# Two recurrent layers in series: the gate biases written by copies instead of products, side work moved between steps, two waits in exchanged order

## The chip, the cores and the metric

The kernel runs on one core of one Trainium2 chip. The metric is device microseconds of one execution, from the first to the last instruction with what lies around them; of several executions the median counts.

## The reference

What must be computed, in float32, with x of 16 batches, 128 time steps and 128 features:

```python
def lstm(x, h0, Wx, Wh, b):            # twice, with weights of its own
    x_proj = einsum('ntd,df->ntf', x, Wx) + b
    def step(carry, xp_t):
        prev_h, prev_c = carry
        h_bar = xp_t + prev_h @ Wh     # four gates of 128
        i, f, o = sigmoid(h_bar[:, :H]), sigmoid(h_bar[:, H:2*H]), sigmoid(h_bar[:, 2*H:3*H])
        g = tanh(h_bar[:, 3*H:])
        next_c = f * prev_c + i * g
        next_h = o * tanh(next_c)
        return (next_h, next_c), next_h
    ...
x = x + attention(lstm(x, cond, ...), W_theta, W_phi, W_g)   # no softmax: theta phi^T scaled, times g
x = x + relu(lstm(x, cond, ...) @ W1 + b1) @ W2 + b2
```

The second layer's input is the first layer's output plus its attention, so the two recurrences of 128 steps each stand one after the other: 256 dependent steps.

## The kernel before

**Layout.** Features lie on the partitions, and the 16 batches of a time step are 16 columns. Eight time steps make a chunk of 128 columns (`CH` = 8); a layer has 16 chunks. Two chunks (16 steps, parities p = 0 and 1) are one turn of a loop: `pe.Fori`, `act.Fori` and `dve.Fori` on the three engines. Layer 1 is eight turns of its loop. Layer 2's first 16 steps are written out (they also carry the rest of the attention), and seven turns follow. In the code t is the step within its chunk and s the step within 16.

**Gate banks.** Each parity has two banks of PSUM: `gibank[p]` holds gates g and i of the chunk's eight steps, `fobank[p]` gates f and o. While the steps of one parity run, the other parity's banks are filled: first the bias by float32 products of a matrix of ones with a 128x512 bias matrix that has the bias in row 0 and zeros below (`bias_gate`, L350 to L353; the products for gates f and g carry start=True), then the input part x @ Wx by one float32 product per gate (`project_gate`, L355 to L358). Each step adds its recurrent part onto the step's 16 columns.

**One step.** TensorE (`step`, L371): a float32 product of the last h (`ring`) with gate f's weights (L387, after h_ready), six half-precision products of `h_hi` and six of `h_lo` for gates g and i (L377), then, after ScalarE has read gate f, six for gate o. ScalarE: sigmoid of f (L662), tanh of g and i (L665), sigmoid of o (L669), tanh of the cell (L672). VectorE: f times the cell (L746), the scan that forms the new cell (L750), h (L753), its half-precision part `h_hi` (L755) and remainder `h_lo` (L758). The scan waits for two things, ScalarE's gates g and i, and VectorE's own product f times the cell:

```python
dve.wait_ge(gi_done[layer], n1)
dve.wait_ge(fc_done[layer], n + 2)
nc.vector.tensor_tensor_scan(out=c_scan, ...)
```

**Side work.** The order on each engine is the order in which the code is written; nothing else schedules. After the 19 products of a step TensorE does that step's piece of other work and then waits for the next h: in layer 1 the transposing of the next chunk's x and the products for values and keys (t = 0), bias products (one at t = 0, three at t = 1), queries (t = 2), input products (one at t = 2, three at t = 3), scores (t = 4), attention (t = 6). In layer 2's loop it is the feed-forward products and, at t = 2, 3, 6 and 7, one bias product and one input product. `keep_warm` (L360) adds dummy half-precision products of 512 columns, as many as the tables say:

```python
WARM1 = [0, 0, 0, 0, 1, 3, 1, 3]
WARM2 = [1, 1, 0, 1, 1, 1, 1, 1]
```

VectorE's side work stands behind L758 of a step (scores L763 at t = 5, a copy L782 at t = 7, in layer 2 relu L809 at t = 2 and 3 and the output L849 at t = 6), ScalarE's behind L672.

**Start.** SyncE loads x, bias and condition of layer 1, ScalarE's queue its weights, GpSimd's queue all of layer 2's, which GpSimd then scales and splits until about 22 us. VectorE scales gate g's part of bias, `Wh` and `Wx` and splits `Wh` (L732 to L741).

## Time and profile before

| | us |
|---|---|
| median of 3 runs (all: 485.89, 489.92, 499.64) | 489.92 |
| the profiled execution | 489.24 |
| its span, first to last instruction | 487.2 |

| engine | busy us | share of the span |
|---|---|---|
| TensorE products | 451.1 | 93% |
| TensorE weight loads | 354.8 | 73% |
| VectorE | 261.3 | 54% |
| ScalarE | 212.8 | 44% |
| GpSimd | 17.4 | 4% |

The times of a row are start and duration in microseconds from the span's start. A float32 product of 128 columns stands in the trace as two records of weight load and two of product, so "x4" is two products. Products overlap in the array: their starts tell how long it is taken, their durations do not. "PEld" is the weight load, "PE" the product, "DVEq" VectorE's own queue (waits and register arithmetic), and what stands in brackets is the idle time of the engine ahead of the row and who ended it. The granted clock reads 1.00 in every stretch of this trace.

### The profile page before, as it was taken

How to read it: one execution, taken by the hardware profiler on the slowest of the kernel's cores; microseconds unless marked ns; L12 is line 12 of the kernel's file. 1: busy time of each engine (PE TensorE's matmuls, PEld its weight loads, DVE VectorE, ACT ScalarE, POOL GpSimd, SP SyncE). 2: the span in 40 equal slices, each digit the busy share in tenths (PEclk: the TensorE clock that was granted, in tenths of full speed). 3: DMA queues.
4: the chain of work that ended last, by engine and by line, in shares of the span. 5: the costliest groups of instructions: out<-in, count | busy, mean ns of one | idle time of the engine just before them, and what ended most of it. 6: DMA issues, size and time to landing. Idle time of an engine off the chain costs nothing.

```text
span 487.2 us, 16863 instructions
## 1 busy us (share of the span) xinstructions
PE 451.1 (93%) x6350; PEld 354.8 (73%) x6440; DVE 261.3 (54%) x1422; ACT 212.8 (44%) x1092; POOL 17.4 (4%) x29
## 2 busy tenths in 40 slices
PE   8999999999999999999999999999999999999997
PEld 6876677766667776667789977777777777777775
DVE  4445554555555455555545655555555555555554
ACT  1434445444454444444435344444444444444443
POOL 6700000000000000000000000000000000000000
PEclk9999999999999999999999999999999999999999
DMA  5001111001111100110000000000000000000000
GB/s 160 7 3 17 16 16 16 14 3 16 16 16 16 16 11 5 16 16 11 11 12 3 7 18 18 18 16 12 4 16 16 16 16 16 11 5 16 16 16 11
DMA packets 11690, 8.12 MB, mean 17 GB/s; under 512 B 1098, under 2 KB 11130, under 8 KB 11675
## 3 DMA queue, kind: packets, MB, share of 16 engines
q1 hardware_dynamic: 10874, 6.17, 6.4%
q0 software_dynamic: 512, 1.22, 0.8%
q10 hardware_dynamic: 288, 0.52, 0.4%
q8 instruction: 10, 0.16, 0.2%
q14 instruction: 6, 0.04, 0.0%
HBM read 2.87 MB, written 1.05 MB: 8 GB/s over the span
## 4 chain that ended last, share of the span: by engine, by line
PE 60%; DVE 16%; ACT 14%; issue 7%; DVEq 1%; DMA 1%; ACTq 0%
PE fobank L387 20%; PE gibank L377 16%; DVE cell L750 10%; ACT scan L665 8%; DVE ring L753 6%; ACT cell L672 6%; PE fobank L377 5%; PE gibank L352 3%; PE fobank L352 3%; PE gibank L357 3%; PE fobank L357 2%; PE bankY L431 2%; DVEq L749 1%; PE bankY L535 1%; DMA x_rows<-in_x_dram 1%
## 5 line engine op out<-in xcount | busy, mean ns | idle before, releaser
L387 PEld LDWEIGHTS fobank<-ring,whf 128*128 128x128 f32 x510 | 78.3, 192 | 96.7 <-DVE ring L753 96.3
L387 PE MATMUL fobank<-ring,whf 128*128 128x16 f32 x510 | 100.1, 272 | 28.5 <-DVE ring L753 19.0
L662 ACT ACTIVATE fgate<-fobank 128x16 f32<-128x16 f32 x256 | 47.2, 184 | 167.6 <-PE fobank L387 165.3
L750 DVE TENSOR_TENSOR_SCAN cell<-scan 128x48 f32<-128x48 f32 x256 | 69.1, 270 | 56.2 <-ACT scan L665 53.1
L746 DVE TENSOR_TENSOR scan<-fgate,cell 128x16 f32<-128x16 f32 x256 | 45.4, 177 | 90.4 <-ACT fgate L662 88.4
L377 PEld LDWEIGHTS gibank<-h_hi,wh_parts 128*128 128x128 bf16 x1536 | 79.6, 111 | 0.0
L753 DVE SCALAR_TENSOR_TENSOR ring<-cell,ogate 128x16 f32<-128x16 f32 x256 | 44.7, 175 | 60.0 <-ACT cell L672 60.0
L377 PE MATMUL gibank<-h_hi,wh_parts 128*128 128x16 f16 x1536 | 75.5, 169 | 0.0
L377 PE MATMUL gibank<-h_lo,wh_parts 128*128 128x16 f16 x1536 | 75.4, 169 | 0.0
L665 ACT ACTIVATE scan<-gibank 128x32 f32<-128x32 f32 x256 | 54.9, 215 | 27.9
L672 ACT ACTIVATE cell<-cell 128x16 f32<-128x16 f32 x256 | 43.0, 168 | 40.6 <-DVE cell L750 38.8
L377 PE MATMUL fobank<-h_hi,wh_parts 128*128 128x16 f16 x771 | 60.0, 174 | 0.4 <-ACT fgate L662 0.2
L377 PEld LDWEIGHTS gibank<-h_lo,wh_parts 128*128 128x128 bf16 x1536 | 56.6, 96 | 0.0
L377 PE MATMUL fobank<-h_lo,wh_parts 128*128 128x16 f16 x768 | 56.2, 169 | 0.0
L669 ACT ACTIVATE ogate<-fobank 128x16 f32<-128x16 f32 x256 | 47.1, 184 | 19.9 <-PE fobank L377 0.5
L377 PEld LDWEIGHTS fobank<-h_hi,wh_parts 128*128 128x128 bf16 x771 | 36.2, 97 | 19.5 <-ACT fgate L662 0.5
L758 DVE TENSOR_TENSOR h_lo<-ring,h_hi 128x16 f16<-128x16 f32 x256 | 45.2, 176 | 8.7
L755 DVE SCALAR_TENSOR_TENSOR h_hi<-cell,ogate 128x16 f16<-128x16 f32 x256 | 42.2, 165 | 0.0
L377 PEld LDWEIGHTS fobank<-h_lo,wh_parts 128*128 128x128 bf16 x768 | 37.4, 96 | 0.0
L363 PE MATMUL bankU<-warm_x,warm_w 128*128 128x512 bf16 x96 | 29.7, 392 | 1.3 <-issue 0.2
L352 PE MATMUL fobank<-ones,bias 128*128 128x128 f32 x136 | 28.6, 293 | 0.0
L352 PE MATMUL gibank<-ones,bias 128*128 128x128 f32 x136 | 27.7, 310 | 0.0
(150 smaller groups left out, 467.8 us busy)
## 6 DMA issues: line engine op xcount, KB each, us to landing
rows_t<-rows SPq DMA_DIRECT2D x16, 128.0 KB
x_rows<-in_x_dram SPq DMA_DIRECT2D x17, 64.0 KB
out_dram<-y_sb SPq DMA_DIRECT2D x16, 64.0 KB
xres<-x2T SPq DMA_DIRECT2D x15, 64.0 KB, 1.9
xin<-x2T SPq DMA_DIRECT2D x14, 64.0 KB, 1.8
w<-in_L_ffn_W_dram POOLq DMA_DIRECT2D x2, 256.0 KB, 3.9
wh<-in_L_cond_Wh_dram ACTq DMA_DIRECT2D x1, 256.0 KB, 2.8
wx<-in_L_cond_Wx_dram ACTq DMA_DIRECT2D x1, 256.0 KB, 3.7
```

What stands on the lines that cost most here:

```text
L352: return nc.tensor.matmul(gate_out(p, g), bias[layer][:, gate_cols(g)], moving(ones[:, :], g), start=g in (GF, GG), stop=False, skip_group ...
L377: last = nc.tensor.matmul(step_out(p, t, g), wh_parts[layer][:, part, gate_cols(g)], h[:, (s - 1) % STEPS, :], start=False, stop=True, ski ...
L387: nc.tensor.matmul(step_out(p, t, GF), whf[layer][:], ring[:, (s - 1) % STEPS, :], start=False, stop=True, skip_group_check=True).then_inc ...
L662: nc.scalar.activation(fgate[:], fobank[p][:, NB * t:NB * t + NB], ACT.Sigmoid).then_inc(f_done[layer], 1)
L665: nc.scalar.activation(gi_slots, gibank[p][:, 2 * NB * t:2 * NB * (t + 1)].rearrange("p (g b) -> p g b", g=2), ACT.Tanh, scale=0.5).then_i ...
L669: nc.scalar.activation(ogate[:], fobank[p][:, P + NB * t:P + NB * t + NB], ACT.Sigmoid).then_inc(tanh_done[layer], 1)
L672: nc.scalar.activation(tanhc, c_psum, ACT.Tanh, scale=0.5).then_inc(tanh_done[layer], 1)
L746: nc.vector.tensor_tensor(out=fc_slots, in0=fgate[:], in1=c_psum, op=ALU.mult).then_inc(fc_done[layer], 1)
L750: nc.vector.tensor_tensor_scan(out=c_scan, data0=scan_mul, data1=scan_add, initial=0.0, op0=ALU.mult, op1=ALU.add).then_inc(c_ready[layer], 1)
L753: nc.vector.scalar_tensor_tensor(out=ring[:, s, :], in0=tanhc, scalar=H_UNIT, in1=ogate[:], op0=ALU.mult, op1=ALU.mult).then_inc(h_ready[l ...
L755: nc.vector.scalar_tensor_tensor(out=h_hi[:, s, :], in0=tanhc, scalar=H_UNIT, in1=ogate[:], op0=ALU.mult, op1=ALU.mult).then_inc(hi_ready[ ...
L758: nc.vector.tensor_tensor(out=h_lo[:, s, :], in0=ring[:, s, :], in1=h_hi[:, s, :], op=ALU.subtract).then_inc(lo_ready[layer], 1)
```

## The change

Bias: the two matrices of 128x512 become two of 128x4, one column a gate (order g, i, f, o), loaded by two DMAs each (`load_bias`), layer 1's on SyncE's queue with no clearing ahead, layer 2's on GpSimd's. `bias_gate`, `ones` and all bias products are gone. In their place VectorE writes the bias into the other parity's banks with two copies of 128x256 from SBUF to PSUM (`seed_gi`, `seed_fo`), and TensorE's input products wait for them (`seeded`). Where they stand: layer 1 behind steps t = 1 and t = 2; layer 2's loop behind t = 0 and t = 1; in the written-out 16 steps both behind step 1 and both behind step 11; before each layer's first step, both. The four dummy products at the start now write the gate banks.

Side work on TensorE: in layer 1 the products for values and keys move from t = 0 to t = 1 and the input products from t = 2 (one) and t = 3 (three) to t = 3 (two) and t = 5 (two). In the written-out steps the four input products at step 12 move to steps 13 (one), 14 (one) and 15 (two). `WARM1` and `WARM2` are the same.

The scan's two waits stand in the other order.

```diff
@@ VectorE, step @@
                 nc.vector.tensor_tensor(out=fc_slots, in0=fgate[:], in1=c_psum,
                                         op=ALU.mult).then_inc(fc_done[layer], 1)
+                dve.wait_ge(fc_done[layer], n + 2)
                 dve.wait_ge(gi_done[layer], n1)
-                dve.wait_ge(fc_done[layer], n + 2)
                 nc.vector.tensor_tensor_scan(out=c_scan, data0=scan_mul, data1=scan_add, initial=0.0,
...
@@ VectorE, new functions and the loop of layer 1 @@
+            def seed_gi(layer, p):
+                nc.vector.tensor_copy(gibank[p][:, 0:2 * P].rearrange("p (t g b) -> p t g b", g=2, b=NB),
+                                      bias[layer][:, 0:2].unsqueeze(1).unsqueeze(3).broadcast_to([P, CH, 2, NB])
+                                      ).then_inc(seeded[layer], 1)
+            def seed_fo(layer, p):
+                nc.vector.tensor_copy(fobank[p][:, 0:2 * P].rearrange("p (g n) -> p g n", g=2),
+                                      bias[layer][:, 2:4].unsqueeze(2).broadcast_to([P, 2, P])
+                                      ).then_inc(seeded[layer], 1)
...
+                    if t == 1:
+                        seed_gi(0, 1 - p)
+                    if t == 2:
+                        seed_fo(0, 1 - p)
...
@@ VectorE, before the first step @@
-            dve.wait_ge(bias1_loaded, 16)
-            nc.vector.tensor_scalar(bias[0][:, gate_cols(GG)], ...)
+            dve.wait_ge(bias1_loaded, 32)
+            nc.vector.tensor_scalar(bias[0][:, 0:1], bias[0][:, 0:1], 2.0, None, ALU.mult).then_inc(bias_ready, 1)
+            dve.wait_ge(gate_banks_opened, 1)
+            dve.wait_ge(bias_ready, 1)
+            seed_gi(0, 0)
+            seed_fo(0, 0)
             dve.wait_ge(wh1_loaded, 16)
...
@@ loads @@
+        def load_bias(eng, layer, b, done):
+            eng.dma_start(bias[layer][:, 1:4], b[0:3 * H].rearrange("(g p) -> p g", p=P), ...).then_inc(done, 16)
+            eng.dma_start(bias[layer][:, 0:1], b[3 * H:4 * H].unsqueeze(1), ...).then_inc(done, 16)
...
@@ TensorE, loop of layer 1 @@
+                    if t == 1:
                         pe.wait_ge(rows_kept, i * 2 + (p + 1))
                         row_products(1 - p, bankY)
-                    if t in (0, 1):
-                        for g in (GATES[0:1], GATES[1:])[t]:
-                            bias_gate(0, 1 - p, g)
...
+                    if t in (3, 5):
+                        if t == 3:
+                            pe.wait_ge(seeded[0], i * 4 + (2 * p + 4))
+                        rhs = xT[:, bass.ds(i * 2 + (p + 1), 1), :].rearrange("p c n -> p (c n)")
+                        for g in {3: GATES[0:2], 5: GATES[2:4]}[t]:
+                            project_gate(0, 1 - p, g, rhs)
...
-                    if t in (2, 3):
-                        rhs = ...
-                        for g in (GATES[0:1], GATES[1:])[t - 2]:
-                            project_gate(0, 1 - p, g, rhs)
...
@@ TensorE, layer 2, written-out steps @@
-                if s in (8, 9, 10, 11):
-                    bias_gate(1, 0, GATES[s - 8])
...
-                    for g in GATES:
+                if s in (13, 14, 15):
+                    if s == 13:
+                        pe.wait_ge(seeded[1], 6)
+                    for g in {13: GATES[0:1], 14: GATES[1:2], 15: GATES[2:4]}[s]:
                         last = project_gate(1, 0, g, x2T[:, 2, :])
...
@@ TensorE, loop of layer 2 @@
                         g = {2: GF, 3: GG, 6: GI, 7: GO}[t]
-                        bias_gate(1, 1 - p, g)
+                        if t == 2:
+                            pe.wait_ge(seeded[1], i * 4 + (2 * p + 4))
                         last = project_gate(1, 1 - p, g, xin[:, 1 - p, :])
```

**The scan's waits, in VectorE's row.** A wait is either a part of the instruction it stands with or an instruction of its own ahead of it. The kernel before, a looped step of layer 1 (`cell<-scan` is the scan, REGISTER_ALU the arithmetic for a wait's value):

```order
L758 TENSOR_TENSOR h_lo<-ring,h_hi 128x16 [waits hi_ready1]
L746 TENSOR_TENSOR scan<-fgate,cell 128x16 [waits f_done1]
L749 REGISTER_ALU [waits gi_done1]
L750 SCALAR_TENSOR_TENSOR cell<-scan 128x48 [waits fc_done1]
L752 ISA
L753 SCALAR_TENSOR_TENSOR ring<-cell,ogate 128x16 [waits tanh_done1]
```

The changed kernel, behind step t = 1 of layer 1:

```order
L767 TENSOR_TENSOR h_lo<-ring,h_hi 128x16 [waits hi_ready1]
L715 COPY gibank<-bias 128x256
L755 TENSOR_TENSOR scan<-fgate,cell 128x16 [waits f_done1]
L757 REGISTER_ALU
L759 SCALAR_TENSOR_TENSOR cell<-scan 128x48 [waits gi_done1,fc_done1]
L761 ISA
L762 SCALAR_TENSOR_TENSOR ring<-cell,ogate 128x16 [waits tanh_done1]
```

Before, the register arithmetic (L749) waits for gates g and i, and the scan for f times the cell. Now the arithmetic waits for nothing, and two waits stand with the scan. Of two in such a list the first named is an instruction of its own ahead (L758, a bare semaphore wait) and the last is the scan's own: it is again f times the cell. In the written-out steps of the kernel before the list is the other way round:

```order
L758 TENSOR_TENSOR h_lo<-ring,h_hi 128x16 [waits hi_ready2]
L763 TENSOR_TENSOR scores<-bankY,same_batch 128x256 [waits scores_ready]
L746 TENSOR_TENSOR scan<-fgate,cell 128x16 [waits f_done2]
L750 SCALAR_TENSOR_TENSOR cell<-scan 128x48 [waits fc_done2,gi_done2]
L753 SCALAR_TENSOR_TENSOR ring<-cell,ogate 128x16 [waits tanh_done2]
```

and in the changed kernel it is as in the loop:

```order
L767 TENSOR_TENSOR h_lo<-ring,h_hi 128x16 [waits hi_ready2]
L772 TENSOR_TENSOR scores<-bankY,same_batch 128x256 [waits scores_ready]
L755 TENSOR_TENSOR scan<-fgate,cell 128x16 [waits f_done2]
L759 SCALAR_TENSOR_TENSOR cell<-scan 128x48 [waits gi_done2,fc_done2]
L762 SCALAR_TENSOR_TENSOR ring<-cell,ogate 128x16 [waits tanh_done2]
```

So outside the loop the wait for gates g and i moves from the scan itself to an instruction ahead of it.

**TensorE at t = 5 of layer 1.** Before, from the step's last products for gate o to the next step's first product:

```order
L377 MATMUL fobank<-h_hi,wh_parts 128x16 x2
L377 MATMUL fobank<-h_lo,wh_parts 128x16 x3
L363 MATMUL bankU<-warm_x,warm_w 128x512 x3
L386 REGISTER_ALU
L387 MATMUL fobank<-ring,whf 128x16 [waits h_ready1]
```

And now:

```order
L373 MATMUL fobank<-h_hi,wh_parts 128x16 x2
L373 MATMUL fobank<-h_lo,wh_parts 128x16 x3
L353 MATMUL gibank<-xT,wx 128x8x16
L353 MATMUL fobank<-xT,wx 128x128
L359 MATMUL bankU<-warm_x,warm_w 128x512 x3
L382 REGISTER_ALU
L383 MATMUL fobank<-ring,whf 128x16 [waits h_ready1]
```

Two input products now stand ahead of the three dummy ones.

## Rows read from the trace of the kernel before

**Rows 1.** The page, part 4: the chain that ended last, shares by engine
```profile
PE 60%; DVE 16%; ACT 14%; issue 7%; DVEq 1%; DMA 1%; ACTq 0%
```

**Rows 2.** Timeline, a looped step of layer 1 (start us, us, what)
```profile
104.77 0.17 DVE L753 SCALAR_TENSOR_TENSOR ring<-cell,ogate 128x16 f32<-128x16 f32 x1 [0.23 <-ACT cell L672]
...
105.00 0.30 PEld L387 LDWEIGHTS fobank<-ring,whf 128*128 128x128 f32 x2 [0.18 <-DVE ring L753]
...
105.65 0.18 DVE L746 TENSOR_TENSOR scan<-fgate,cell 128x16 f32<-128x16 f32 x1 [0.41 <-ACT fgate L662]
...
105.81 0.52 PEld L352 LDWEIGHTS gibank<-ones,bias 128*128 128x128 f32 x4
...
106.06 0.27 DVE L750 TENSOR_TENSOR_SCAN cell<-scan 128x48 f32<-128x48 f32 x1 [0.23 <-ACT scan L665]
...
106.26 0.30 PEld L352 LDWEIGHTS fobank<-ones,bias 128*128 128x128 f32 x2
...
106.56 0.17 DVE L753 SCALAR_TENSOR_TENSOR ring<-cell,ogate 128x16 f32<-128x16 f32 x1 [0.23 <-ACT cell L672]
...
106.79 0.30 PEld L387 LDWEIGHTS fobank<-ring,whf 128*128 128x128 f32 x2 [0.23 <-DVE ring L753]
```

**Rows 3.** Source line L749, VectorE's queue: duration ns min/median/max, first and last start
```profile
L749 DVEq ALU_OP  x233: 40/40/52, 13.8 to 481.1; - x117
L749 DVEq EVENT_SEMAPHORE  x23: 21/21/21, 251.0 to 479.3; - x23
```

**Rows 4.** Chain in order of time, a looped step (start us, us, what)
```profile
112.88 0.22 ACT scan L665
...
113.14 0.04 DVEq L749
...
113.22 0.28 DVE cell L750
```

**Rows 5.** Chain in order of time, a step of layer 2 outside the loop
```profile
254.24 0.22 ACT scan L665
...
254.48 0.28 DVE cell L750
```

**Rows 6.** Chain in order of time, the last products and the last copy
```profile
483.16 0.96 PE bankY L531 x8
...
484.15 0.02 DVEq L855
...
484.22 0.29 DVE y_sb L856
```

**Rows 7.** Timeline, layer 1, the step with t = 5
```profile
112.99 0.81 PE L363 MATMUL bankU<-warm_x,warm_w 128*128 128x512 bf16 x3
113.95 0.30 PEld L387 LDWEIGHTS fobank<-ring,whf 128*128 128x128 f32 x2 [0.64 <-DVE ring L753]
```

**Rows 8.** Timeline, layer 2, step 12 outside the loop: two results
```profile
276.48 0.17 DVE L753 SCALAR_TENSOR_TENSOR ring<-cell,ogate 128x16 f32<-128x16 f32 x1 [0.23 <-ACT cell L672]
...
278.40 0.17 DVE L753 SCALAR_TENSOR_TENSOR ring<-cell,ogate 128x16 f32<-128x16 f32 x1 [0.23 <-ACT cell L672]
```

**Rows 9.** Groups by line and shape (busy us, mean ns | idle before)
```profile
L763 DVE TENSOR_TENSOR scores<-bankY,same_batch 128x256 f32<-128x256 f32 x17 | 7.2, 425 | 0.0
```

**Rows 10.** Timeline, VectorE, early steps of layer 1
```profile
20.15 0.17 DVE L753 SCALAR_TENSOR_TENSOR ring<-cell,ogate 128x16 f32<-128x16 f32 x1 [0.23 <-ACT cell L672]
...
22.17 0.17 DVE L753 SCALAR_TENSOR_TENSOR ring<-cell,ogate 128x16 f32<-128x16 f32 x1 [0.23 <-ACT cell L672]
...
24.49 0.17 DVE L753 SCALAR_TENSOR_TENSOR ring<-cell,ogate 128x16 f32<-128x16 f32 x1 [0.23 <-ACT cell L672]
```

**Rows 11.** Timeline, before the first step
```profile
5.82 0.55 PEld L352 LDWEIGHTS fobank<-ones,bias 128*128 128x128 f32 x2 [0.28 <-issue]
...
8.08 0.50 PEld L357 LDWEIGHTS fobank<-xT,wx 128*128 128x128 f32 x2
```

**Rows 12.** DMA issues by line (KB, us from issue to landing)
```profile
b<-in_L_ffn_b_dram POOLq DMA_DIRECT2D x1, 2.0 KB, 3.5
```

More of the change, by code:

```diff
@@ L75, in build @@
         ident = sb("ident", [P, P])
-        ones = sb("ones", [P, P])
         wx = [sb(f"wx{n}", [P, 4 * H]) for n in (1, 2)]
         wh = [sb(f"wh{n}", [P, 4 * H]) for n in (1, 2)]
-        bias = [sb(f"bias{n}", [P, 4 * H]) for n in (1, 2)]
+        bias = [sb(f"bias{n}", [P, 4]) for n in (1, 2)]
         cond_rows = sb("cond_rows", [NB, H])
@@ L224, in start_h @@
             nc.vector.memset(c_psum, 0.0).then_inc(fc_done[layer], 1)
+        def load_bias(eng, layer, b, done):
+            eng.dma_start(bias[layer][:, 1:4], b[0:3 * H].rearrange("(g p) -> p g", p=P),
+                          allow_slow_non_contiguous=True).then_inc(done, 16)
+            eng.dma_start(bias[layer][:, 0:1], b[3 * H:4 * H].unsqueeze(1),
+                          allow_slow_non_contiguous=True).then_inc(done, 16)
         @block.sync
@@ L229, in _ @@
             sp.dma_start(x_rows[:, 0, :], x_ctb[0]).then_inc(rows_loaded[0], 16)
-            sp.wait_ge(bias1_cleared, 1)
-            sp.dma_start(bias[0][0:1, :], l1_b.unsqueeze(0)).then_inc(bias1_loaded, 16)
+            load_bias(sp, 0, l1_b, bias1_loaded)
             sp.dma_start(cond_rows[:], cond).then_inc(cond_loaded, 16)
@@ L304, in _ @@
             pool.dma_start(wg_rows[:], w_g).then_inc(attn_w_loaded, 16)
-            nc.gpsimd.memset(bias[1][:], 0.0).then_inc(bias2_cleared, 1)
-            pool.wait_ge(bias2_cleared, 1)
-            pool.dma_start(bias[1][0:1, :], l2_b.unsqueeze(0)).then_inc(weights2_loaded, 16)
+            load_bias(pool, 1, l2_b, weights2_loaded)
             pool.dma_start(wx[1][:], l2_wx).then_inc(weights2_loaded, 16)
@@ L315, in _ @@
             nc.gpsimd.memset(x2T[:, NCH, :], 0.0).then_inc(set2_ready, 1)
-            pool.wait_ge(weights2_loaded, 112)
-            for w in (wx[1], wh[1], bias[1]):
-                nc.gpsimd.tensor_scalar(w[:, gate_cols(GG)], w[:, gate_cols(GG)], 2.0, None,
-                                        ALU.mult).then_inc(set2_ready, 1)
+            pool.wait_ge(weights2_loaded, 128)
+            for w in (wx[1][:, gate_cols(GG)], wh[1][:, gate_cols(GG)], bias[1][:, 0:1]):
+                nc.gpsimd.tensor_scalar(w, w, 2.0, None, ALU.mult).then_inc(set2_ready, 1)
             nc.gpsimd.tensor_scalar(w1[:], w1[:], 1.0 / H_UNIT, None, ALU.mult).then_inc(set2_ready, 1)
@@ L348, in moving @@
                 return tile if g in (GF, GO) else tile.rearrange("p (t b) -> p t b", b=NB)
-            def bias_gate(layer, p, g):
-                return nc.tensor.matmul(gate_out(p, g), bias[layer][:, gate_cols(g)], moving(ones[:, :], g),
-                                        start=g in (GF, GG), stop=False, skip_group_check=True)
             def project_gate(layer, p, g, tile):
@@ L399, in _ @@
             pe.wait_ge(consts_ready, 1)
-            keep_warm(bankV, 4)
+            for bank in (gibank[0], fobank[0], gibank[1], fobank[1]):
+                last = nc.tensor.matmul(bank[:, :], warm_w[:], warm_x[:], start=True, stop=True, skip_group_check=True)
+            last.then_inc(gate_banks_opened, 1)
             pe.wait_ge(consts_ready, 2)
@@ L477, in _ @@
             pe.wait_ge(set2_ready, SET2)
-            for g in GATES:
-                bias_gate(1, 0, g)
             last_keys = ring[:, CH:STEPS, :].rearrange("p t b -> p (t b)")
@@ L544, in _ @@
                     score_products(P, hist[:, 0, :], P, P).then_inc(scores_ready, 1)
-                if s == 1:
-                    for g in GATES:
-                        bias_gate(1, 1, g)
                 if s == 2:
@@ L576, in _ @@
                     residual(x2T[:, 0, :])
-                    for g in GATES:
+                if s in (13, 14, 15):
+                    if s == 13:
+                        pe.wait_ge(seeded[1], 6)
+                    for g in {13: GATES[0:1], 14: GATES[1:2], 15: GATES[2:4]}[s]:
                         last = project_gate(1, 0, g, x2T[:, 2, :])
+                if s == 15:
                     last.then_inc(x2_projected, 1)
@@ L784, in _ @@
                                               ).then_inc(hist_done, 1)
+            dve.wait_ge(set2_ready, SET2)
+            seed_gi(1, 0)
+            seed_fo(1, 0)
             dve.wait_ge(scores_ready, NCH + 1)
@@ L816, in _ @@
                     keep_scores(2 * P)
+                if s == 1:
+                    seed_gi(1, 1)
+                    seed_fo(1, 1)
                 if s == 2:
@@ L820, in _ @@
                     late_x2(s - 7)
+                if s == 11:
+                    seed_gi(1, 0)
+                    seed_fo(1, 0)
                 if s == 12:
@@ L837, in _ @@
                     c = i * 2 + p
+                    if t == 0:
+                        seed_gi(1, 1 - p)
+                    if t == 1:
+                        seed_fo(1, 1 - p)
                     if t == 2:
```

15 lines of the change are left out of this document (5 added, 10 removed).

## The prediction, made before the changed kernel ran

> **What bounds the kernel now.** I read the chain that ended last first: TensorE has 60% of it, VectorE 16%, ScalarE 14% [rows 1]. That a busy engine is also the bound is not said by this, so the timeline of one step came next. From one h (L753) to the next the step takes 1.79 us, 104.77 to 106.56 [rows 2], and the reader is to see two things in it. The load for L387 stood idle for 0.23 us until VectorE's h came, though three bias products had been made in that step; so TensorE waits for h even in a full step. And the scan L750 stood idle for 0.23 us until ScalarE's gates g and i came. The ring h, L387, gates, scan, tanh, h is the bound, and side work is not, as long as it fits between gate o's products and the next h. Reading all results of L753 in order, 119 of layer 1's steps and 105 of layer 2's are 1.79 us long. So 0.01 us in the ring is worth over 2 us, and 50 us of products outside it are worth nothing.
>
> **The change, part by part.**
>
> *The scan's waits.* In a looped step ScalarE's gates end at 113.10, the register arithmetic that waits for them starts at 113.14 and the scan at 113.22: 0.12 us from gates to scan [rows 4]. Outside the loop, where the scan itself waits for the gates and a bare wait ahead of it takes the other semaphore, it is 254.46 to 254.48, 0.02 to 0.03 us [rows 5]. After the change it is neither: a bare wait for the gates, then the scan. This combination the trace shows at the end, for the last copy: the products end at 484.12, the bare wait starts at 484.15, the copy at 484.22, which is 0.10 us [rows 6]. The queue's durations say the same: 40 ns for the arithmetic, 21 ns for a bare wait, a difference of 0.019 us [rows 3]. That arithmetic stood there 233 times: 233 x 0.019 = 4.4 us gained. The other 23 steps (16 written out, one in each of 7 turns) had the good form and lose it: 0.10 - 0.03 = 0.07 us in about 18 of them, while in about 5 the product f times the cell comes last and gains as much: 1.3 - 0.4 = 0.9 us lost. Sum -3.5 us. Bounds: nothing gained in the 233 and all 23 lost, +1.6; or the gates' wait as fast as in rows 5, -21.
>
> *Bias products.* All of them go. In rows 2 the three took TensorE from 105.81 to about 106.48, and the next load waited for h all the same: worth 0 in the loops. The cover was the wait itself, so nothing is uncovered either.
>
> *The copies.* A copy of 128x256 with PSUM on one side: the nearest row is the product for the scores, 0.43 us of the same size [rows 9]. It stands behind L758, where VectorE has 0.41 us of idle time before L746 [rows 2], so L746 starts at most a few hundredths late; L746 ends 0.23 us before the scan starts (105.83, 106.06) [rows 2], and the scan's own wait for it needs 0.03 of that. Up to about 0.6 us a copy costs 0. In the written-out steps 1 and 11 two stand in a row: 0.86 us, L746 0.45 late, of which 0.2 is slack: +0.25 each, +0.5 us. From below: a copy like the fastest of its size, 0.3 us, gives 0.
>
> The Trainium skill (VectorE: DVE Perf Modes, section "Why PSUM operands drop a tier") says that a float32 operation with a PSUM operand gets no double rate. The trace's 0.43 us agrees as an estimate of one element a cycle. By the double rate the copies would take some 0.3 us and these 0.5 us would be 0.
>
> *Layer 1's step t = 5.* The input products move behind three dummy products' step. Before, the dummies took TensorE from 112.99, some 0.215 us each (0.81 us with the last one's tail), and the next step's load began at 113.95 [rows 7]. Two float32 products take 0.45 us more (105.81 to 106.26 for two) [rows 2]: the array is free at 112.99 + 0.45 + 0.64 = 114.08, against a load that would now start at 113.93 and may run beside the last dummy for some 0.1 us. So 0.05 to 0.15 us. The nearest row of a step with five such pieces is step 12 outside the loop, 1.92 us [rows 8], against 1.70 for its neighbours, which had less; that was a float32 tail, whose loads are longer. I take 0.1: 16 x 0.1 = +1.6 us; bounds 0 and 16 x 0.22 = 3.5. In no other step is there more than three pieces, and four fitted at 1.70.
>
> *The first steps.* Step times there: 20.15 to 22.17 is 2.02 us, with the side work hidden; 22.17 to 24.49 is 2.32 us with three input products [rows 10]. The products' durations there are twice those of later stretches, the lower level of TensorE's two, though the granted clock reads 1.00. Steps 1 and 3 go from three pieces to two (-0.3 each), step 0 from three and a half to a transposing (-0.6), step 5 from three to five at twice 0.215 (+0.86): -0.4 us. GpSimd's operations stall VectorE here now and then, up to 0.8 us, and where they fall then cannot be said: bounds -2 and +1.
>
> *Before the first step.* The bias products run from 5.82 on, the input products start at 8.08 [rows 11]. Now the latter wait for the copies. Layer 1's bias comes in single elements; layer 2's b1, of 2 KB in single elements too, took 3.5 us from issue to landing [rows 12]. Issued at about 1.6 and 2.3, the bias is there at 5.8; doubling gate g's column, two copies (0.86), then `Wh` and `Wx` scaled: the input products start at about 7.4, -0.7 us. Bounds: -1.5, and +2 if the load takes 2.7 us longer, since nothing else would cover it.
>
> *Between the layers and in the written-out steps.* Before the second layer the products with h0 now wait for two copies behind the last h, where bias products filled TensorE: +0.35 us. Steps 8 to 11 lose one bias product each behind attention products that keep TensorE busy: 0.22 to 0.3 us in three of them, -0.8 us. Bounds -1.5 and +1 for both.
>
> *Sum.* -3.5 + 0 + 0.5 + 1.6 - 0.4 - 0.7 + 0.35 - 0.8 = -2.95 us. The profiled execution took 489.24 us (its span 487.2 and 2.0 around it), so 486.3 us. The three runs' median is 0.14% above that execution: 487.0 us. One per cent is 4.9 us; a measurement of this kernel tells about 2% from no change.
>
> **Rivals.**
>
> *The clock falls in layer 1's light steps (slower).* Before, each step had three pieces of side work of 0.215 to 0.22 us; now layer 1's t = 0 to 3 have half a piece, two, two and two, 7 us in a row of lighter work in each chunk. If TensorE falls to 1.2 GHz in them and comes back in the full steps t = 5 to 7, then t = 2 and 3 cost 2.02 instead of 1.79 [rows 10, 2], t = 4 about 2.4, t = 5 about 2.95, t = 6 about 2.33: up to 2.7 us a chunk, 43 us in 16. If only two light steps are hit, 0.46 x 16 = 7 us. That is 494 to 530, with 510 in between; from 0.6 us a chunk on it decides. For it: the early steps, which are full of products, still ran at the lower level until about 31 us, so rising is not easy. Against: no stretch after that fell, and some of those had gaps too.
>
> The Trainium skill (TensorE: Matmul & The Clock Gate, section "A second HAM failure mode: psum-queue depth-cycling") tells of a kernel whose frequent small gaps between groups made the clock swing between its two levels; by that the rival is right. The same page's section "Loop structure matters more than you think" ties the fall to long idle waits, which this kernel has not; by that it is wrong. No row here is as light as the new steps, so the trace bears out neither.
>
> *The exchange gives its full worth (faster).* If a wait ahead of the scan cost no more than the scan's own, the 0.12 would become 0.03: 233 x 0.09 = 21 us, so 469 us with the other terms. Rows 5 speak for it, but there the late semaphore was the scan's own; rows 6 have the new order and say 0.10.
>
> *The bias arrives late.* With the load's bound of +2 us and a stall of GpSimd's, 490 us: no measurable change either.
>
> **How the numbers follow.** The forecast has 0.68, with its own range of 482 to 492; the falling clock 0.22, of which 0.03 stay under 2%; the full exchange 0.05; the late bias 0.05. The range for all, 479 to 508, leaves out the full exchange and the worse half of the falling clock. Faster by over 2% (below 480): 0.06. Slower by over 2% (above 499.7): 0.19. Between: 0.75.
>
> **What would show it.** Right: the scan starts 0.10 us after ScalarE's gates in every step, looped steps are 1.77 us long, t = 5 of layer 1 1.85 to 1.9, L753 to L387's load keeps its idle time, copies last about 0.43 us and L746 is not followed by a late scan. Wrong: scans 0.03 us behind the gates (469); product durations of the light steps twice as long (over 494); scans that wait for L746; a first step that starts later than before.

## The result and the profile after

The changed kernel takes 572.23 us (median of 4 runs, 570.54 to 576.49) against 490.14 for the kernel before beside it: 1.174 times as long, 95% interval 1.164 to 1.185. The forecast was 487.0 with a range of 479 to 508. The profiled execution took 572.85 us, its span 570.7. Throughout, a time is the median of all executions of a kernel, while a ratio leaves out those in a slower state of the chip, so the two can differ by some tenths of a per cent.

The page of the changed kernel: busy time, granted clock in 40 slices, and the chain by engine.

```profile
PE 546.1 (96%) x6168; PEld 443.0 (78%) x6168; DVE 286.5 (50%) x1488; ACT 211.8 (37%) x1092; POOL 17.1 (3%) x29
PEclk9997756557756557756688675555556655556656
PE 88%; DVE 5%; ACT 3%; issue 2%; DMA 1%; DVEq 0%; ACTq 0%
```

Before, PEclk was 9 in all slices and TensorE had 60% of the chain [rows 1]. Now TensorE runs mostly at the lower of its two levels (1.2 GHz; 5 in this line) and has 88%: the ring is no longer the only bound, TensorE's own products are.

Where the 83.5 us lie (570.7 - 487.2) is read from four results h each: the first, the first of layer 2's written-out steps, the first of its loop, the last. First before, then after.

```profile
14.41 0.17 DVE L753 SCALAR_TENSOR_TENSOR ring<-cell,ogate 128x16 f32<-128x16 f32 x1 [0.23 <-ACT cell L672]
...
251.57 0.17 DVE L753 SCALAR_TENSOR_TENSOR ring<-cell,ogate 128x16 f32<-128x16 f32 x1 [0.23 <-ACT cell L672]
...
283.60 0.18 DVE L753 SCALAR_TENSOR_TENSOR ring<-cell,ogate 128x16 f32<-128x16 f32 x1 [0.23 <-ACT cell L672]
...
481.69 0.17 DVE L753 SCALAR_TENSOR_TENSOR ring<-cell,ogate 128x16 f32<-128x16 f32 x1 [0.23 <-ACT cell L672]
```

```profile
13.75 0.17 DVE L762 SCALAR_TENSOR_TENSOR ring<-cell,ogate 128x16 f32<-128x16 f32 x1 [0.23 <-ACT cell L668]
...
291.52 0.17 DVE L762 SCALAR_TENSOR_TENSOR ring<-cell,ogate 128x16 f32<-128x16 f32 x1 [0.23 <-ACT cell L668]
...
327.57 0.17 DVE L762 SCALAR_TENSOR_TENSOR ring<-cell,ogate 128x16 f32<-128x16 f32 x1 [0.23 <-ACT cell L668]
...
564.45 0.17 DVE L762 SCALAR_TENSOR_TENSOR ring<-cell,ogate 128x16 f32<-128x16 f32 x1 [0.23 <-ACT cell L668]
```

Layer 1 with the hand-over: 277.77 against 237.16, +40.6. Written-out steps: 36.05 against 32.03, +4.0. Layer 2's loop: 236.88 against 198.09, +38.8. The rest +0.1.

How it comes in one chunk of layer 1: the changed kernel's windows from one h to the next; the side work of t = 0 stands in the first, that of t = 5 begins in the sixth and reaches into the last (length; busy time of PE, PEld, DVE, ACT, POOL; granted clock; DMA).

```profile
64.10:65.87 1.77, 1.24 (x22) 0.88 (x21) 1.05 (x7) 0.75 (x4) 0.00 (x0) 1.00 0.00 0
65.87:67.64 1.77, 1.51 (x22) 1.03 (x22) 0.87 (x5) 0.78 (x5) 0.00 (x0) 1.00 0.00 0
67.64:69.64 2.00, 1.77 (x22) 1.49 (x22) 1.22 (x7) 1.02 (x6) 0.00 (x0) 0.54 0.00 0
69.64:71.63 1.99, 1.99 (x25) 1.71 (x24) 1.21 (x7) 1.03 (x6) 0.00 (x0) 0.50 0.10 18
71.63:73.62 1.99, 1.99 (x25) 1.84 (x25) 0.88 (x5) 1.00 (x5) 0.00 (x0) 0.50 0.59 80
73.62:75.95 2.33, 2.33 (x26) 1.91 (x25) 0.88 (x5) 0.75 (x4) 0.00 (x0) 0.50 0.01 1
75.95:79.13 3.18, 3.18 (x28) 2.33 (x27) 1.23 (x7) 0.75 (x4) 0.00 (x0) 0.50 0.00 0
```

At t = 0 TensorE is busy for 1.24 of 1.77 us, at t = 1 for 1.51, then the clock falls. From there its own products fill the steps, and the five pieces of t = 5 make the last window 3.18 us long. In the kernel before the fullest and the lightest step of a chunk are these:

```profile
104.77:106.56 1.79, 1.79 (x29) 1.53 (x27) 0.88 (x5) 0.76 (x5) 0.00 (x0) 1.00 0.00 0
...
111.93:113.72 1.79, 1.56 (x23) 0.95 (x23) 0.88 (x6) 0.75 (x4) 0.00 (x0) 1.00 0.16 13
```

TensorE's waits for h in these steps are short. Its loads for the ring at t = 0, 1 and 2:

```profile
64.33 0.30 PEld L383 LDWEIGHTS fobank<-ring,whf 128*128 128x128 f32 x2 [0.62 <-DVE ring L762]
66.09 0.30 PEld L383 LDWEIGHTS fobank<-ring,whf 128*128 128x128 f32 x2 [0.82 <-DVE ring L762]
67.87 0.50 PEld L383 LDWEIGHTS fobank<-ring,whf 128*128 128x128 f32 x2 [0.66 <-DVE ring L762]
```

The same in groups: the load of `whf` for the ring (190 ns at the higher level, in fill_all below) takes half as long again, the dummy products more than a third (392 ns in the kernel before, last line below); the copies are as forecast.

```profile
L383 PEld LDWEIGHTS fobank<-ring,whf 128*128 128x128 f32 x510 | 132.6, 293 | 89.2 <-DVE ring L762 73.2
...
L359 PE MATMUL bankU<-warm_x,warm_w 128*128 128x512 bf16 x129 | 57.0, 536 | 0.0
...
L715 DVE COPY gibank<-bias 128x256 f32<-128x256 f32 x34 | 14.3, 421 | 0.1
```

```profile
L363 PE MATMUL bankU<-warm_x,warm_w 128*128 128x512 bf16 x96 | 29.7, 392 | 1.3 <-issue 0.2
```

What the change did to the scan's waits answers to [rows 4]: the chain of the changed kernel in a looped step.

```profile
65.06 0.22 ACT scan L661
65.28 0.03 issue
65.30 0.02 DVEq L758
65.33 0.04 issue
65.37 0.28 DVE cell L759
```

The gates end at 65.28, the scan starts at 65.37: 0.09 to 0.10 us, where it was 0.12.

### The profile page after: what moved, and what is told of

It is laid out like the page before. It is cut to its first block, busy times and chain, and to the rows that moved or that the text cites. A ratio compares the mean times of both kernels' runs of the same rounds, so it can differ in the third digit from the quotient of the medians.

```text
span 570.7 us, 16742 instructions
## 1 busy us (share of the span) xinstructions
PE 546.1 (96%) x6168; PEld 443.0 (78%) x6168; DVE 286.5 (50%) x1488; ACT 211.8 (37%) x1092; POOL 17.1 (3%) x29
## 4 chain that ended last, share of the span: by engine, by line
PE 88%; DVE 5%; ACT 3%; issue 2%; DMA 1%; DVEq 0%; ACTq 0%
PE fobank L383 14%; PE gibank L373 14%; PE fobank L373 11%; PE bankV L359 7%; PE bankU L359 7%; PE gibank L353 6%; PE fobank L353 6%; PE bankY L526 6%; PE bankU L519 5%; PE bankY L432 3%; PE bankU L453 3%; DVE cell L759 2%; PE bankV L437 2%; ACT scan L661 2%; DVE ring L762 2%
## 5 line engine op out<-in xcount | busy, mean ns | idle before, releaser
L383 PEld LDWEIGHTS fobank<-ring,whf 128*128 128x128 f32 x510 | 132.6, 293 | 89.2 <-DVE ring L762 73.2
L383 PE MATMUL fobank<-ring,whf 128*128 128x16 f32 x510 | 119.7, 314 | 16.9 <-DVE ring L762 15.2
L373 PEld LDWEIGHTS gibank<-h_hi,wh_parts 128*128 128x128 bf16 x1536 | 101.5, 129 | 0.0
L373 PE MATMUL gibank<-h_lo,wh_parts 128*128 128x16 f16 x1536 | 77.9, 173 | 0.4 <-DVE h_lo L767 0.4
L373 PE MATMUL fobank<-h_hi,wh_parts 128*128 128x16 f16 x771 | 63.4, 179 | 0.2 <-ACT fgate L658 0.2
L359 PE MATMUL bankV<-warm_x,warm_w 128*128 128x512 bf16 x104 | 62.5, 604 | 0.0
L373 PEld LDWEIGHTS gibank<-h_lo,wh_parts 128*128 128x128 bf16 x1536 | 59.7, 102 | 0.5 <-DVE h_lo L767 0.5
L359 PE MATMUL bankU<-warm_x,warm_w 128*128 128x512 bf16 x129 | 57.0, 536 | 0.0
L373 PEld LDWEIGHTS fobank<-h_hi,wh_parts 128*128 128x128 bf16 x771 | 40.1, 107 | 16.4 <-ACT fgate L658 0.3
L526 PE MATMUL bankY<-w,relu 128*128 128x128 f32 x128 | 36.7, 441 | 0.0
```

Of the source, the lines that this page charges most:

```text
L359: nc.tensor.matmul(bank[:, :], warm_w[:], warm_x[:], start=True, stop=True)
L373: last = nc.tensor.matmul(step_out(p, t, g), wh_parts[layer][:, part, gate_cols(g)], h[:, (s - 1) % STEPS, :], start=False, stop=True, ski ...
L383: nc.tensor.matmul(step_out(p, t, GF), whf[layer][:], ring[:, (s - 1) % STEPS, :], start=False, stop=True, skip_group_check=True).then_inc ...
L526: return nc.tensor.matmul(bankY[:, 0:D], relu[:, j, :], w2[:, j, :], start=False, stop=(j == NJ - 1))
```

## The experiments

All 17 kernels compute the whole reference; what is added or left out are dummy products and clearings, whose results nobody reads, and the form of a wait. Each ratio is to the kernel before, run beside it; us of a ratio are taken at 487. The granted clock is told by windows of the span; those of all runs stand in a table at the end.

**fill_both, fill_1, fill_2: is it the clock, and where?** Dummy products come back where bias products went.

```diff
 # these four lines: fill_both, fill_1
 t == 0:  +keep_warm(bankU, 2)
 t == 1:  +keep_warm(bankY, 1)
 t == 2:  +keep_warm(bankU, 1)
 t == 3:  +pe.wait_ge(rows_kept, i * 2 + (p + 2)); keep_warm(bankY, 1)
 # this line: fill_both, fill_2
-WARM2 = [1, 1, 0, 1, 1, 1, 1, 1]
+WARM2 = [1, 1, 1, 2, 1, 1, 2, 2]
```

> The changed kernel, and nothing taken back, with dummy products added where bias products were dropped: in layer 1 two more at t = 0 and one more at each of t = 1, 2 and 3; in layer 2 one more at each of t = 2, 3, 6 and 7. Theory (the 83 us come from TensorE's lower clock, and that from the lighter steps): the granted clock reads about 1.00 again, looped steps are 1.77 us, the time is 484 to 489 us. Rival A (the copies into the gate banks, or a wait for them, slow the ring whatever the clock does): the time stays above 540 us. Rival B (the clock falls because of t = 5 with its five pieces or of gaps before h, not of light steps): clock stays under 0.9 and the time above 520 us.

> The changed kernel with the dummy products of fill_both in layer 1's steps only; layer 2's steps stay as light as the change made them. Theory (each layer's own light steps pull the clock down): layer 1 at 1.00 with steps of 1.77 us, layer 2 at about 0.57 as in the changed kernel: 487 + some 105 x 0.38 = about 527 us, 520 to 535. Rival (layer 2 fell only because the clock was already low when it began, its own steps would hold it): under 495 us.

> The changed kernel with one dummy product more in layer 2's t = 2, 3, 6 and 7 only; layer 1 and the written-out steps stay as light as the change made them. Theory (each stretch pays for its own light steps): layer 1 and the written-out steps run mostly at the lower level as in the changed kernel, layer 2's loop at 1.00 and 1.77 us: 572 less the 38 us that the loop loses in fill_1 against fill_both = about 534, 526 to 542. Rival (once low, the clock doesn't come back in layer 2 though its steps are full): over 560.

Measured: fill_both 492.22 us, 1.013 (1.005 to 1.020); fill_1 529.82 us, 1.093 (1.086 to 1.099); fill_2 538.65 us, 1.107 (1.100 to 1.114). Some 78 us of 83 are gone once work that nobody needs is back. Each layer pays for itself: layer 2's filling is worth (1.093 - 1.013) x 487 = 39 us, layer 1's (1.107 - 1.013) x 487 = 46, and the stages above had lost 38.8 and 40.6 + 4.0. The copies and the waits for them are all still in fill_both, so rival A falls; so does rival B, whose five pieces at t = 5 are there too. The lines of PEclk, fill_both, fill_1 and fill_2:

```profile
PEclk9999999999999999999965589999999999999999
```

```profile
PEclk9899999999999999999898555555565556655656
```

```profile
PEclk9977556576657755756675598999999999999999
```

fill_both was expected at 484 to 489; a low stretch is left, at some 246 to 287 us: the hand-over and the written-out steps. These 16 steps take 41.23 us there and 36.05 in the changed kernel, by the same code, so what a light stretch costs isn't a fixed sum.

**fill_all, fill_all_t5: the rest, and the change at an even clock.** Both have fill_both's dummy products and these besides.

```diff
+keep_warm(bankU, 4)                    # before the hand-over's scores
+if s == 1: pe.wait_ge(rows0_kept, 1); keep_warm(bankU, 3)
 s == 12:  +keep_warm(bankV, 2)
-if s >= 13: keep_warm(bankV, 1 + 2 * (s == 15))
+if s >= 13: keep_warm(bankV, 2)
-WARM1 = [0, 0, 0, 0, 1, 3, 1, 3]       # fill_all_t5 alone
+WARM1 = [0, 0, 0, 0, 1, 1, 1, 3]
```

> fill_both, with dummy products also where the change left the hand-over and the written-out steps of layer 2 light: four before the hand-over's scores, three in step 1, two in step 12, two in each of steps 13 to 15. Theory (fill_both's clock fell at about 247 us because that stretch too had become lighter): clock 1.00 throughout, about 10 us less than fill_both: 480 to 484 us, level with the kernel that only exchanges the waits. Rival (the stretch fell for another reason, the wait for the copies behind the last h or the products of float32): the clock falls there again, 490 to 494.

> fill_all with one dummy product in place of three at layer 1's t = 5, so that its step has three pieces and not five. Theory (forecast: the two extra pieces cost 0.1 us a chunk at the higher level; the trace of fill_both shows 1.91 against 1.77, 0.14): t = 5 goes to 1.77 us, 2.2 us less than fill_all: ratio to before about 0.995. Rival (that step becomes one light step too many): the clock falls in part of layer 1, over 490 us.

Measured: fill_all 488.06 us, 0.999 (0.995 to 1.004), where 480 to 484 was expected and swap_only (below) has 0.993; the profiled execution took 484.66 us (span 482.5), clock 1.00 in all slices. fill_all_t5 485.29 us, 0.999 (0.995 to 1.003): two pieces less at t = 5 can't be told from none, and its profiled run lost the clock for a stretch in the written-out steps (0.83 from 240 to 290 us), so its 2 us are not resolved in the time. They are in the trace: the step behind t = 5 reads 1.77 us there. What it costs with five pieces is read from fill_all's h at t = 5 and after it: 224.69, 226.59, 228.36, so 1.90 against 1.77.

```profile
224.69 0.17 DVE L772 SCALAR_TENSOR_TENSOR ring<-cell,ogate 128x16 f32<-128x16 f32 x1 [0.23 <-ACT cell L678]
226.59 0.17 DVE L772 SCALAR_TENSOR_TENSOR ring<-cell,ogate 128x16 f32<-128x16 f32 x1 [0.23 <-ACT cell L678]
228.36 0.17 DVE L772 SCALAR_TENSOR_TENSOR ring<-cell,ogate 128x16 f32<-128x16 f32 x1 [0.23 <-ACT cell L678]
```

The load at the higher level, in the same kernel:

```profile
L383 PEld LDWEIGHTS fobank<-ring,whf 128*128 128x128 f32 x510 | 78.7, 190 | 112.8 <-DVE ring L772 110.1
```

**light_2, dose_1, uneven_2: light steps in the kernel before.** One row is changed, so that t = 3, 6 and 7 of layer 2's loop have two pieces where all had three; or t = 3 alone; or the three, with the pieces moved to t = 0, 1 and 4.

```diff
-WARM2 = [1, 1, 0, 1, 1, 1, 1, 1]
+WARM2 = [1, 1, 0, 0, 1, 1, 0, 0]    # light_2
+WARM2 = [1, 1, 0, 0, 1, 1, 1, 1]    # dose_1
+WARM2 = [2, 2, 0, 0, 2, 1, 0, 0]    # uneven_2
```

> The kernel before, nothing of the change, with one dummy product less in steps t = 3, 6 and 7 of layer 2's looped chunks (0.2 us of TensorE's work in each, none of it on the way to h). Theory (light steps alone do it): layer 2's granted clock falls below 0.8, its steps to 2.0 to 2.4 us, the time is 505 to 535 us, layer 1 unchanged. Rival (products outside the ring are worth nothing, and what fell was something else of the change): 488 to 491 us, clock 1.00.

> The kernel before with one dummy product less in one step of eight of layer 2's loop, t = 3, so that t = 3 has two pieces and every other step three. Theory A (a light step now and then is enough): the clock falls in part of layer 2, 495 to 520 us. Theory B (it takes several light steps in a row or near each other): 486 to 490, clock 1.00.

> The kernel before, layer 2's loop with as many dummy products as before (six in eight steps plus the one moved: 2, 2, 0, 0, 2, 1, 0, 0 where it was 1, 1, 0, 1, 1, 1, 1, 1), so that t = 3, 6 and 7 are as light as in light_2, and t = 0, 1 and 4 have four pieces. Theory A (light steps pull the clock down wherever the rest stands): as light_2, 505 to 535 us. Theory B (what counts is the work over the whole chunk): clock 1.00, 486 to 491 us.

Measured: light_2 521.67 us, 1.075 (1.067 to 1.083); dose_1 509.26 us, 1.043 (1.035 to 1.052); uneven_2 509.87 us, 1.037 (1.027 to 1.046). PEclk of light_2 and of dose_1:

```profile
PEclk9979999999999999999999995675555955655569
```

```profile
PEclk9699999999999999999999999555596989557969
```

One dummy product of 0.2 us less in every eighth step costs 21 us in a kernel that has nothing else of the change. Work elsewhere in the chunk doesn't make up for it (uneven_2), though it lessens the loss.

**swap_only, own_wait: the scan's waits.** In own_wait the count of gi_done starts 3 higher, so that a new value is worked out between the two waits: that arithmetic takes the wait for the product f times the cell, and the scan itself the one for the gates.

```diff
 # swap_only                            # own_wait, looped steps
-dve.wait_ge(gi_done[layer], n1)        -dve.wait_ge(gi_done[layer], n1)
 dve.wait_ge(fc_done[layer], n + 2)      dve.wait_ge(fc_done[layer], n + 2)
+dve.wait_ge(gi_done[layer], n1)        +dve.wait_ge(gi_done[layer], n + 4)
                                         # after start_h: +dve.sem_inc(gi_done[layer], 3)
```

> The kernel before with the scan's two waits exchanged and nothing else. Step by step forecast: 0.12 us between gates and scan become 0.10 in 233 steps, 23 steps lose 0.07: -3.5 us, 486.6. Rival A (full worth, 0.03 us as in the written-out steps): 469. Rival B (nothing, or a loss in the written-out steps alone): 490 to 491.5.

> The kernel before, where the scan in the looped steps waits itself for the gates (register arithmetic ahead of it takes the wait for the product f times the cell), in place of the arithmetic waiting for the gates; nothing else. Theory (what counts is which wait the scan itself has): 0.12 us between gates and scan become 0.03, steps 1.70 us, 233 x 0.09 = 21 us less: 465 to 469. Rival (the next thing to be late fills the gap: the product f times the cell, or the dummy products that reach up to the next h): steps stay at 1.75 or more, over 480.

Measured: swap_only 481.98 us, 0.993 (0.989 to 0.998), so -3.3 us (-5.4 to -1.2). own_wait 467.06 us, 0.955 (0.947 to 0.963), so -22 us. It beats both kernels. Its gates and scans (ScalarE, then VectorE):

```profile
322.49 0.21 ACT L665 ACTIVATE scan<-gibank 128x32 f32<-128x32 f32 x1
```

```profile
321.03 0.27 DVE L755 TENSOR_TENSOR_SCAN cell<-scan 128x48 f32<-128x48 f32 x1
...
321.53 0.18 DVE L758 SCALAR_TENSOR_TENSOR ring<-cell,ogate 128x16 f32<-128x16 f32 x1 [0.23 <-ACT cell L672]
...
322.74 0.27 DVE L755 TENSOR_TENSOR_SCAN cell<-scan 128x48 f32<-128x48 f32 x1
...
323.24 0.17 DVE L758 SCALAR_TENSOR_TENSOR ring<-cell,ogate 128x16 f32<-128x16 f32 x1 [0.23 <-ACT cell L672]
```

From 322.71 to 322.74 is 0.03 us, and from h to h 1.71.

**Fewer products, or more idle time?** own_dose_1 and own_light_2 are own_wait with the rows of dose_1 and light_2. gap_2 and gap_2b leave all products and put a clearing on VectorE before h in layer 2's looped steps; own_gap_light_2 is own_light_2 with that clearing.

```diff
 dve.wait_ge(tanh_done[layer], n * 2 + 2)
+if layer == 1 and not isinstance(n, int):
+    nc.vector.memset(spare[:], 0.0)     # 128x16 in gap_2, 128x128 in the others
```

> own_wait with dose_1's one light step (t = 3 of layer 2's loop has two pieces, the others three). With own_wait's steps of 1.70 TensorE's idle time before each h is 0.09 us shorter, so over eight steps it is 0.7 us shorter, and the piece left out adds 0.2 us of it in one. Theory A (what counts is how long TensorE stands idle over several steps): the clock holds at 1.00, the time is that of own_wait, 464 to 470. Theory B (what counts is the work of a single step): the clock falls in part of layer 2 as in dose_1, 478 to 495.

> The kernel before, all its products in place, with a clearing of a spare tile (128x16) on VectorE between tanh and h in each of the 112 looped steps of layer 2: h comes some 0.06 to 0.1 us later, and TensorE stands idle that much longer in every step. Theory A (TensorE's idle time over several steps is what pulls the clock down): besides the 7 to 11 us of the clearing itself the clock falls in layer 2's loop, over 505 us. Theory B (it is the number of products in a step): clock 1.00, steps of 1.85 to 1.9 us, 493 to 498.

> own_wait with light_2's three light steps of eight (t = 3, 6 and 7 of layer 2's loop with two pieces). Over eight steps the pieces left out add 0.6 us of idle time and own_wait's shorter steps take 0.7 us away. Theory A (idle time over several steps): the clock holds or falls only here and there, 464 to 475. Theory B (three light steps of eight are too many at any length of the ring): the clock falls as in light_2, over 490.

> gap_2 with a clearing of 128x128 in place of 128x16 (in gap_2 the 0.07 us of it ran beside the step and h came no later, so that it told nothing). Before's clearing of this size takes 0.165 us; about 0.1 of it should stand before h in each of the 112 looped steps of layer 2. Theory A (TensorE's idle time over several steps pulls the clock down, with every product in place): clock below 0.95 in layer 2, over 510 us. Theory B (products missing are what does it): clock 1.00, steps of 1.88 us, 484 + 112 x 0.1 = 494 to 498.

> own_light_2 (own_wait's wait and three light steps of eight in layer 2, whose clock held) with gap_2b's clearing before h in layer 2, so that its steps are about 1.79 us again, by another cause than the wait's form. Theory A (idle time): the clock falls in layer 2 as in light_2, over 495 us. Theory B (something in the form of the wait holds the clock): clock 1.00, 465 + 112 x 0.1 = 474 to 479.

Measured: own_dose_1 464.29 us, 0.956 (0.949 to 0.962), and own_light_2 465.08 us, 0.957 (0.948 to 0.967): both hold the clock, without the same products whose absence cost the kernel before 21 and 36 us. gap_2 486.71 us, 1.003 (0.998 to 1.007), told nothing: the clearing ran beside h's own start.

```profile
320.87 0.15 DVE L756 SCALAR_TENSOR_TENSOR ring<-cell,ogate 128x16 f32<-128x16 f32 x1 [0.26 <-issue]
320.88 0.07 DVE L755 MEMSET spare<- 128x16 f32 x1
```

gap_2b 504.20 us, 1.032 (1.024 to 1.039), with every product in place: the steps at the higher level are 1.86 us (rows below) and not 1.79, some 8 us in 112, and the other 7 of its 15 are the clock's. The expected 510 was too high; the clock falls in short stretches.

```profile
289.11 0.11 DVE L756 SCALAR_TENSOR_TENSOR ring<-cell,ogate 128x16 f32<-128x16 f32 x1
...
290.97 0.11 DVE L756 SCALAR_TENSOR_TENSOR ring<-cell,ogate 128x16 f32<-128x16 f32 x1
```

```profile
PEclk9969999999999999999999989988899869888999
```

own_gap_light_2 513.39 us, 1.050 (1.042 to 1.058): with its idle time back, own_light_2 loses the clock. First own_light_2, then own_gap_light_2.

```profile
PEclk9989999999999999999999999999999999999999
```

```profile
PEclk9999999999999999999999965855558555555865
```

So the clock falls when TensorE has less work for the length of its steps, whether a product is taken away or h comes later; in these two kernels a shorter ring gave room for lighter steps. That it is TensorE's idle time before h, summed over neighbouring steps, is the account I went by, and it is argued, not shown. The traces' own idle time doesn't sort the runs: over eight looped steps of layer 2 TensorE is shown idle for 1.17 us of 14.32 in the kernel before, which held its clock throughout, and for 1.01 of 14.30 in own_gap_light_2 just before it fell. (The ends of products in the rows are modelled, so this idle time is rough.) First the kernel before, then own_gap_light_2.

```profile
312.15:326.47 14.32, 13.15 (x198) 10.49 (x201) 8.18 (x46) 6.00 (x32) 0.00 (x0) 1.00 0.05 15
```

```profile
281.59:295.89 14.30, 13.29 (x199) 10.39 (x198) 8.19 (x54) 5.98 (x32) 0.00 (x0) 1.00 0.05 13
```

**mended, after_own: the change with own_wait's wait.** mended has it beside fill_all_t5's products (layer 1's dummy product of t = 3 behind the input products); after_own has it alone.

> The change as it could be: fill_all_t5 with layer 1's dummy product of t = 3 behind the input products (no wait ahead of these), and own_wait's form of the scan's waits. Theory (the copies in place of bias products are worth nothing on the ring, neither gain nor loss, and the wait is worth its 20 us): as own_wait, 462 to 468, ratio to before 0.95 to 0.96. Rival (the copies or the new order take part of the gain with the shorter step): 470 to 480.

> The changed kernel, no product put back, with own_wait's form of the scan's waits: looped steps are 0.07 us shorter than the change's 1.77, so TensorE's idle time before h falls by 0.6 us in eight steps, against four products of 0.2 us that layer 2 lost in eight steps and some five pieces in layer 1. Theory (idle time summed over neighbouring steps): over the kernel before, layer 2 has 0.8 - 0.7 = 0.1 us more of it in eight steps, layer 1 about 1 - 0.7 = 0.3: the clock falls in parts of both, least in layer 2: 475 to 530. Rival A (the missing products count by themselves): nearly as the change, over 545. Rival B (the shorter step saves it all): clock 1.00, about 466.

Measured: mended 470.69 us, 0.967 (0.963 to 0.972), near own_wait but not under it. The time missed 462 to 468 and lies in the rival's range: its steps are 1.70 us too, but a stretch at the lower level about the written-out steps is left (0.90 from 240 to 290; the 16 take 33.23 us against 31.94), and layer 2's loop takes 191.26 us against 189.62, which isn't explained. after_own 569.55 us, 1.161 (1.154 to 1.169): the shorter steps save next to nothing of the change. Here my sum of idle time failed (475 to 530), and rival A, that the missing products count by themselves, gave the time. Layer 2's loop began at the higher level and lost it for the rest (0.50 from 337 to 562):

```profile
328.42:337.30 8.88, 8.25 (x123) 6.34 (x122) 5.94 (x32) 3.75 (x20) 0.00 (x0) 0.97 0.07 18
337.30:360.29 22.99, 22.99 (x265) 19.76 (x265) 11.85 (x63) 8.25 (x44) 0.00 (x0) 0.50 0.06 16
```

Its loop differs from own_light_2's, which held, by one product more gone (t = 2), by the copies, and by the lower level in what ran before it. Which of these tips it isn't known; none was tried alone.

Granted clock from 30 to 240 us, 240 to 290 and 290 to 460. In the faster kernels these are roughly layer 1, the hand-over with the written-out steps, and layer 2's loop. In three the stages come later: layer 1 lasts until about 286 us and layer 2's loop begins at 327.57 (changed), 331.23 (fill_2) and 328.42 (after_own). By its stages the changed kernel has 0.68, 0.76 and 0.55, and fill_2's loop 1.00. The row of uneven_2 is of an execution of 512.01 us, one of its longer ones.

| kernel | 30-240 | 240-290 | 290-460 |
|---|---|---|---|
| changed | 0.66 | 0.64 | 0.60 |
| fill_1 | 1.00 | 0.93 | 0.54 |
| fill_2 | 0.62 | 0.64 | 0.94 |
| fill_both | 1.00 | 0.62 | 1.00 |
| fill_all, swap_only, gap_2 | 1.00 | 1.00 | 1.00 |
| fill_all_t5 | 1.00 | 0.83 | 1.00 |
| light_2, dose_1, uneven_2 | 1.00 | 1.00 | 0.64, 0.72, 0.74 |
| own_wait, own_dose_1, own_light_2 | 1.00 | 1.00 | 1.00 |
| gap_2b | 0.99 | 1.00 | 0.89 |
| own_gap_light_2 | 1.00 | 1.00 | 0.58 |
| mended | 1.00 | 0.90 | 1.00 |
| after_own | 0.64 | 0.61 | 0.59 |

## Why the prediction was wrong

**The step that failed is "Bias products ... worth 0 in the loops. The cover was the wait itself, so nothing is uncovered either."** On the ring they were worth 0, as fill_all shows. But they gave TensorE work while it waited for h, and with that they kept its clock. The 83 us are lost with them, and some 78 come back with dummy products in their place. In layer 2's loop nothing was moved, only the bias products went, and it lost 38.8 us; in layer 1 side work was moved as well, and what each of the two did there wasn't tried alone. The end of the prediction's first paragraph, that 50 us of products outside the ring are worth nothing, is the same error: light_2 takes 0.6 us in eight steps of such work away and loses 36 us.

**The rival was named and given too little.** "The clock falls in layer 1's light steps" is what happened. Its prices held, nearly: t = 3 at 2.02 us (1.99), t = 4 at 2.4 (2.33), t = 5 at 2.95 (3.18), 43 us for layer 1 (40.6, with the hand-over). That the sums agree so well is in part luck: t = 1 was slow too (2.00 in the median chunk), and t = 6 mostly not (1.77, where 2.33 stood). Two things went wrong. It looked at layer 1 alone, though layer 2 lost a product in each of t = 2, 3, 6 and 7: another 38.8 us. And it had 0.22 because "no stretch after that fell, and some of those had gaps too". But each of those stretches had three pieces in every step, so they said nothing of lighter ones, as the text itself admitted: "the trace bears out neither". With a price ten times that of all other terms, an unknown of this kind had to widen the range.

Of the two sections of the Trainium skill (TensorE: Matmul & The Clock Gate) that were weighed, "A second HAM failure mode: psum-queue depth-cycling" is the one that these runs bear out: the clock fell with short waits alone, of 0.62 to 0.82 us. "Loop structure matters more than you think" names only the long wait, and by it the clock would have held; the loads for the ring stood idle for no longer than that before it fell.

**The terms, at an even clock.**
- Waits, -3.5 us: right; swap_only measured -3.3 (-5.4 to -1.2). The middle form costs 0.10 us as [rows 6] said. The bound of -21 is real, but takes other code, in which the scan itself waits for the gates: own_wait, -22 us.
- Copies, nothing in the loops: right. They last 0.42 us, as forecast from [rows 9], and fill_both's loops run at 1.77 us.
- t = 5, 0.1 us a chunk: 0.13 (1.90 against 1.77), 2.1 us where 1.6 stood.
- Written-out steps, -0.8 and the copies' +0.5 there, so -0.3; hand-over, +0.35: fill_all's sixteen written-out steps take 31.99 us and its hand-over 5.56, where swap_only, with the same waits, has 32.34 and 5.52. So -0.35 and +0.04, with fill_all's own dummy products in both: the first as forecast, the second smaller, neither of any weight.
- Before the first step and in the first steps, -0.7 and -0.4: the profiled run's first h came 0.66 us earlier, but that isn't shown to be the change. With before's own products up to there the first h came at 13.06 in swap_only and 14.70 in light_2, and the eight steps after it took 15.1 and 17.9 us; terms this small can't be read from one execution.
- Sum of -2.95: fill_all, which has the change whole with dummy products in the gaps, is at 0.999 (0.995 to 1.004), so -2.4 to +1.8 us. Some 0.8 us in it are fill_all's own wait ahead of the input products at t = 3: in layer 1's chunks that step takes 1.83 us on average, and 1.77 in swap_only.

## What to carry to other kernels

Work that stands beside the critical path isn't free to remove where TensorE is near the edge of its clock: before removing or spreading it, ask of each step what TensorE will do while it waits, in every stage that the change touches, and keep a dummy product for each piece that goes. Shortening the ring gives time and some room: here the form of one wait on VectorE was worth 22 us, and with it one or three lighter steps of eight in layer 2 did no harm. It isn't a protection to count on: it saved next to nothing of the whole change (after_own). When a rival's price is ten times the sum of all terms and no row bears on it, the range has to hold it; one altered constant, as in dose_1, shows whether it is real.

## What the hardware showed that was not expected

- The fall is steep: one product of 0.2 us less in eight steps of 1.79 us cost 21 us (dose_1), and layer 2's loop went to a granted clock of 0.72 (290 to 460 us).
- A TensorE that is shown busy throughout can stay at the lower level. In fill_1's loop of layer 2 PE is shown busy for all of 30 us at 0.50. The ends of products are modelled, and the loads show that in three steps of eight it still waited for h; what it would do without any wait, this run doesn't show. First the window, then one of these loads:

```profile
330.00:360.00 30.00, 30.00 (x340) 25.70 (x339) 16.31 (x85) 10.52 (x57) 0.00 (x0) 0.50 0.05 13
```

```profile
341.76 0.50 PEld L383 LDWEIGHTS fobank<-ring,whf 128*128 128x128 f32 x2 [0.42 <-DVE ring L767]
```

- Between gates and scan, one dependence costs 0.12, 0.10 or 0.03 us by how its wait stands: taken by register arithmetic ahead, by a bare wait ahead, or by the scan itself.
- A clearing of 128x16 before h, 0.07 us long, took no time at all (gap_2), one of 128x128, 0.165 us long, made the steps 0.07 to 0.08 longer (gap_2b): about half of its time stood beside other work.
